# A new, finer step order in a software-pipelined graph network kernel, and another PSUM bank for the product with V

## What is computed

```
h = relu(layernorm(x));  x = x + L0(h)   # 8 Euler steps of a diffusion, folded into a polynomial
h = relu(layernorm(x));  x = x + L1(h)   # graph attention (gat): softmax over masked, leaky s1 + s2, times W h
h = relu(layernorm(x));  x = x + L2(h)   # attention over 256 edges (edge), 4 heads, gather and scatter by node
h = relu(layernorm(x));  x = x + L3(h)   # Laplacian propagation and norm (cheb), masked softmax attention
                                         # with 4 heads of 32 (att), norm, gelu FFN, norm (ffn)
```

## Time and profile before

| | |
|---|---|
| median of 3 runs | 1535.29 us (1531.87 to 1538.79) |
| profiled execution | 1538.55 us, its span 1536.8 us |
| granted TensorE clock, mean | 0.92 |
| busy: PE / DVE / ACT / POOL | 81% / 54% / 50% / 31% |
| layers part of the span | from about 454 us on |

### The profile page before, as it was taken

The page is one execution under the profiler, slowest core; times in us unless marked ns, Lnnn a source line. Parts: engine busy times, 40 slices in busy tenths (PEclk is TensorE's granted clock), DMA queues, the critical chain, the costliest instruction groups (busy, mean ns, idle before and its releaser), DMA issues. The chain is left out here.

```text
span 1536.8 us, 24908 instructions
## 1 busy us (share of the span) xinstructions
PE 1245.7 (81%) x7613; PEld 953.8 (62%) x7613; DVE 834.5 (54%) x2837; ACT 772.1 (50%) x1612; POOL 471.6 (31%) x578
## 2 busy tenths in 40 slices
PE   5899999999964576887887988888878878878754
PEld 3578788888953454665665665666656656655432
DVE  6632131322323456677668677677676676755431
ACT  4124233331102226667667667667676676665651
POOL 5012030113402223325245244244343352442222
PEclk8899999999985788999999999999999999999976
DMA  5010111101010012322312412413313224124210
GB/s 101 14 42 8 43 34 35 49 15 48 1 35 7 14 43 54 90 57 66 99 46 63 109 35 74 105 30 84 75 47 96 55 61 103 43 64 101 67 52 12
DMA packets 123742, 83.62 MB, mean 54 GB/s; under 512 B 13216, under 2 KB 106784, under 8 KB 123680
## 3 DMA queue, kind: packets, MB, share of 16 engines
q1 hardware_dynamic: 123680, 82.82, 21.1%
HBM read 28.25 MB, written 20.97 MB: 32 GB/s over the span
## 5 line engine op out<-in xcount | busy, mean ns | idle before, releaser
L1320 ACT ACTIVATE att_Es<-att_Ts,att_small 128x512 f32<-128x512 f32 x256 | 184.0, 719 | 139.3 <-DVE att_small L1501 130.5
L1501 DVE CUSTOM_DVE_ANT_0 att_Ts<-bank,mask_att 128x512 f32<-128x512 f32 x256 | 174.3, 686 | 132.2 <-PE bank L1568 131.0
L1704 PE MATMUL bank<-ident,att_Es 128*128 128x128 f32 x1024 | 168.5, 290 | 81.7 <-ACT att_PTs L1328 69.6
L1704 PEld LDWEIGHTS bank<-ident,att_Es 128*128 128x128 f32 x1024 | 122.2, 147 | 148.0 <-ACT att_Es L1320 91.3
L1328 ACT COPY att_PTs<-bank 128x512 f32<-128x512 f32 x256 | 145.7, 569 | 18.3 <-PE bank L1704 18.1
L1568 PE MATMUL bank<-K_parts,Q_parts 128*128 128x512 f32 x256 | 133.9, 533 | 3.6 <-DVE att_small L1501 3.6
L289 POOL TENSOR_SCALAR l_rs<-l_mv 128x4 f32<-128x4 f32 x16 | 6.9, 432 | 248.4 <-DVE l_mv L469 248.3
L844 PE MATMUL bank<-G,x0T 128*128 128x128 f32 x384 | 75.9, 280 | 1.2 <-DVE U2T L478 1.0
L483 DVE TENSOR_TENSOR P_row<-bank,l_bias 128x512 f32<-128x512 f32 x32 | 22.1, 691 | 99.2 <-PE bank L854 77.7
L844 PE MATMUL bank<-G,U2T 128*128 128x128 f32 x384 | 75.0, 277 | 0.0
L844 PE MATMUL bank<-G,U1T 128*128 128x128 f32 x384 | 75.0, 277 | 0.0
(11 more groups left out here) (307 smaller groups left out, 3236.0 us busy)
## 6 DMA issues: line engine op xcount, KB each, us to landing
Q_parts<-q_hi SPq DMA_DIRECT2D x128, 64.0 KB, 2.0
Q_parts<-q_lo SPq DMA_DIRECT2D x128, 64.0 KB, 2.0
K_parts<-k_hi SPq DMA_DIRECT2D x128, 64.0 KB, 2.0
K_parts<-k_lo SPq DMA_DIRECT2D x128, 64.0 KB, 2.0
l_x<-in_x SPq DMA_DIRECT2D x16, 256.0 KB, 3.0
P2T<-in_x SPq DMA_DIRECT2D x16, 256.0 KB, 4.2
x_after_l<-P2T SPq DMA_DIRECT2D x16, 256.0 KB, 2.3
gat_xin<-x_after_l SPq DMA_DIRECT2D x16, 256.0 KB, 3.2
```

What stands on the lines that cost most here:

```text
L1320: nc.scalar.activation(att_E[:, j % RING_E, :], att_T[:, j % RING_T, :], ACT.Exp, scale=-1.0, bias=att_small[:, 0, j:j + 1], accum_out=att ...
L1501: nc.vector.tensor_tensor_reduce(att_T[:, j % RING_T, :], [c0, c1][j % 2][:], k.mask_att[:, j % NT, :], -QK_SCALE, HUGE, ALU.add, ALU.min, ...
L1704: mm = nc.tensor.transpose(c2[:, cols(s)], att_E[:, i % RING_E, cols(s)], k.ident[:])
```

## The change

Only `build_layers` is touched. The steps are cut finer: a step that ran several instructions in a row becomes several steps (for example `gat_max` becomes `gat_max0` to `gat_max3`, `edge_max` four steps of one head, `ln_stats` is split into statistics and aggregation, an affine step into its two instructions, and the att steps into att_score, att_turn, att_mask, att_exp and att_copy). A step can carry a `+` in an order: it then works on the batch of one pass earlier, that is, its lag is one more. Splitting brings some waits of its own (`freed`) in front of steps that another step used to stand between. The product with V goes into b0 instead of c2, and the wait of the first transpose for `att_oT` is gone. The cut of the diff:

```diff
 ORDER = {
     "PE": """
-        att16 att0 att1 att17 att18 att2 ffn_wo att3 cheb_prop att4 gat_turn cheb_g gat_wh att5 gat_s2 ffn_turn
-        att6 ffn_up att7 ffn_down att8 gat_eturn0 edge_gather att9 cheb_x1turn gat_eturn2 cheb_q edge_x att10
-        cheb_k edge_lb att11 gat_pv edge_lcol att12 edge_den att13 edge_scatter att14 edge_out att15 cheb_v
+        att_score0 att_score1 att_turn15+ att_rows+ att_pv0+ att_pv1+ att_score2 att_turn0 ffn_wo att_score3
+        att_turn1 cheb_prop0 cheb_prop1 att_score4 att_turn2 gat_turn cheb_g gat_wh gat_s1 att_score5 att_turn3
+        gat_s2 ffn_turn att_score6 att_turn4 ffn_up0 ffn_up1 att_score7 att_turn5 ffn_down0 ffn_down1 att_score8
+        att_turn6 gat_eturn0 gat_eturn1 edge_gather0 edge_gather1 att_score9 att_turn7 cheb_x1turn gat_eturn2
+        gat_eturn3 cheb_q edge_x att_score10 att_turn8 cheb_k edge_lb0 edge_lb1 att_score11 att_turn9 gat_pv0
+        gat_pv1 edge_lcol edge_v att_score12 att_turn10 edge_den att_score13 att_turn11 edge_scatter att_score14
+        att_turn12 edge_out att_score15 att_turn13 cheb_v att_turn14
     "DVE": """
-        cheb_stats att16 edge_stats att0 att1 cheb_lo att_scale att2 gat_stats att3 ffn_y2 gat_apply att4
-        n2_apply cheb_y att5 gat_s1_out att6 gat_scores att7 n1_apply gat_max att8 ffn_y3 cheb_x1 att9 cheb_qlow
-        att10 edge_z cheb_klow edge_max att11 n3_apply edge_le att12 edge_u att13 att14 ffn_final att15 edge_x3
-        gat_x2
+        cheb_stats cheb_aggr gat_x2a+ att_mask0 gat_x2b+ edge_stats att_mask1 edge_aggr cheb_lo att_mask2
+        att_scale gat_stats ffn_y2 gat_aggr att_mask3 n2_stats n2_aggr gat_apply att_mask4 n2_apply cheb_y
+        n1_stats n1_aggr att_mask5 gat_s1_out gat_scores0 att_mask6 gat_scores1 gat_scores2 gat_scores3 gat_row1
+        n1_apply gat_row2 gat_row3 att_mask7 gat_max0 gat_max1 ffn_y3 gat_max2 att_mask8 gat_max3 n3_stats
+        cheb_x1 att_mask9 cheb_qlow edge_z att_mask10 edge_max0 edge_max1 att_mask11 edge_max2 cheb_klow n3_aggr
+        gat_rinv edge_max3 edge_le att_mask12 edge_rden edge_attn edge_u att_mask13 n3_apply att_mask14
+        att_mask15 edge_x3 att_rv ffn_final
     "ACT": """
-        att16 att17 att18 cheb_apply cheb_hi att0 att1 att2 edge_apply att3 cheb_xpT gat_hT att4 edge_hi
-        gat_wh_out att5 ffn_x2T att6 ffn_gelu att7 gat_exp att8 gat_eT0 edge_hg cheb_x1T att9 cheb_qsplit
-        edge_xz gat_eT2 cheb_ksplit att10 att11 edge_exp att12 att13 edge_yT att14 att15 cheb_vout
+        cheb_apply cheb_hi att_spread+ att_exp0 att_exp1 att_exp2 att_copy0 edge_apply att_exp3 att_copy1
+        cheb_xpT edge_hi gat_hT att_exp4 att_copy2 gat_wh_out att_exp5 att_copy3 ffn_x2T att_exp6 att_copy4
+        ffn_gelu0 ffn_gelu1 att_exp7 att_copy5 gat_exp0 gat_exp1 gat_exp2 att_exp8 att_copy6 gat_exp3 gat_eT0
+        gat_eT1 edge_hg cheb_x1T att_exp9 att_copy7 cheb_qsplit edge_xz gat_eT2 gat_eT3 att_exp10 cheb_ksplit
+        att_copy8 att_exp11 att_copy9 edge_exp att_exp12 att_copy10 att_exp13 att_copy11 edge_yT att_exp14
+        att_copy12 att_exp15 att_copy13 cheb_vout att_copy14 att_copy15
     "POOL": """
-        cheb_rstd edge_rstd ffn_res gat_rstd n2_rstd n2_affine n1_rstd ffn_b2 edge_lo gat_low n1_affine n3_rstd
-        n3_affine
+        cheb_rstd edge_rstd ffn_res gat_rstd n2_rstd n2_g n2_b n1_rstd edge_lo ffn_b2 gat_low0 gat_low1 gat_low2
+        gat_low3 n1_g n1_b n3_rstd n3_g n3_b
     "SP": """
-        load_x load_ffn cheb_res load_v stack0 stack2 stack1 stack3 store_out store_v edge_store
+        load_x load_ffn stack1+ stack3+ store_v+ load_v cheb_res edge_store+ stack0 stack2 store_out
...
+            lags = {step: LAG[STAGE_OF[step.rstrip("+")]] + step.count("+") for step in order}
...
         def ln_stats(dve, tag, n, src):
+            freed(dve, tag + "_aggr", n, NT)
...
+        def ln_aggr(dve, tag, n, last_reader):
+            freed(dve, *last_reader)
...
             def att_scale(n):
-                nc.vector.tensor_tensor(oT[:], c2[:], row_scale[:], ALU.mult).then_inc(sem("att_oT"), 1)
+                nc.vector.tensor_tensor(oT[:], b0[:], row_scale[:], ALU.mult).then_inc(sem("att_oT"), 1)
...
-                    if i == 0:
-                        freed(pe, "att_oT", n)
...
+            def att_pv(n, half):
+                if half == 0:
+                    need(pe, sem("edge_done"), min(n + 3, B) if isinstance(n, int) else n + 3)
...
-                            mm = nc.tensor.matmul(c2[r, :], vD[:, s, r], att_PT[:, h, s, :], start=(s == 0),
+                        mm = nc.tensor.matmul(b0[r, :], vD[:, s, r], att_PT[:, h, s, :], start=(s == 0),
```

More of the change, by code:

```diff
@@ L988 @@
     "gat": """
-        load_x gat_rstd gat_stats gat_hT gat_turn gat_apply gat_wh gat_wh_out gat_s2 gat_s1_out gat_scores
-        gat_low gat_exp gat_max gat_eT0 gat_eturn0 gat_eturn2 gat_eT2 gat_pv gat_x2
+        gat_turn gat_wh gat_s1 gat_s2 gat_eturn0 gat_eturn1 gat_eturn2 gat_eturn3 gat_pv0 gat_pv1 gat_stats
+        gat_aggr gat_apply gat_s1_out gat_scores0 gat_scores1 gat_scores2 gat_scores3 gat_row1 gat_row2 gat_row3
+        gat_max0 gat_max1 gat_max2 gat_max3 gat_rinv gat_x2a gat_x2b gat_hT gat_wh_out gat_exp0 gat_exp1
@@ L996 @@
+        edge_x3 edge_apply edge_hi edge_hg edge_xz edge_exp edge_yT edge_rstd edge_lo edge_store
     """.split(),
     "cheb": """
-        cheb_rstd cheb_stats cheb_apply cheb_hi cheb_lo cheb_xpT cheb_res cheb_prop cheb_g stack0 cheb_y
-        stack2 stack1 n1_rstd stack3 n1_apply n1_affine cheb_x1 cheb_x1turn cheb_x1T cheb_q cheb_qsplit
-        cheb_qlow cheb_ksplit cheb_klow cheb_k cheb_vout cheb_v store_v
+        cheb_prop0 cheb_prop1 cheb_g cheb_x1turn cheb_q cheb_k cheb_v cheb_stats cheb_aggr cheb_lo cheb_y
@@ L1003 @@
+    """.split(),
     "ffn": """
-        load_ffn att_scale ffn_res ffn_wo n2_rstd ffn_y2 n2_apply n2_affine ffn_turn ffn_x2T ffn_b2
-        ffn_gelu ffn_up n3_rstd ffn_y3 ffn_down n3_apply store_out n3_affine ffn_final
-    """.split() + [f"att{j}" for j in range(TILES, TILES + 3)],
+        ffn_wo ffn_turn ffn_up0 ffn_up1 ffn_down0 ffn_down1 att_scale ffn_y2 n2_stats n2_aggr n2_apply ffn_y3
+        n3_stats n3_aggr n3_apply ffn_final ffn_x2T ffn_gelu0 ffn_gelu1 ffn_res n2_rstd n2_g n2_b ffn_b2 n3_rstd
+        n3_g n3_b load_ffn store_out
@@ L1656, in edge_out, with cheb_prop @@
                 by_nodes(b1, YT, W["WoutT"][:]).then_inc(sem("edge_outed"), 1)
-            def cheb_prop(n):
-                ready(pe, "cheb_hlo", n)
-                freed(pe, "v_out", n)
-                for s in range(NT):
+            def cheb_prop(n, half):
+                if half == 0:
+                    ready(pe, "cheb_hlo", n)
+                    freed(pe, "v_out", n)
+                for s in (2 * half, 2 * half + 1):
                     for i, (left, right) in enumerate([(h_hi, k.lap_hi), (h_hi, k.lap_lo), (h_lo, k.lap_hi)]):
```

406 lines of the change are left out of this document (227 added, 179 removed).

## The result

The changed kernel takes 1450.67 us (median of 4 runs, 1449.96 to 1454.56), the kernel before 1537.04 beside it. The ratio is 0.9439, with a 95% interval of 0.9395 to 0.9484. The span shrinks by 88.1 us, from 1536.8 to 1448.7. It is outside the narrower band of the forecast (1463 to 1490), which had a chance of 0.5; the case that came is that rival, which had 0.17.

What follows compares the result with a forecast made beforehand. No engine is full: a pass is a chain crossing engines, TensorE nearest to full. 4.3 + 0.4 = 4.7 per pass over twelve passes, 56.4, plus 5 gives 61.4, forecast 1474 us, range 1446 to 1512.

Steps and rivals of the forecast that it cites:

- narrower band of the forecast: Whole kernel: the forecast case, 1463 to 1490 us, with a chance of 0.5.
- that rival: TensorE's clock stays up and slack in VectorE's block is used: 5.8 to 6.3 per pass, 1455 us; chance 0.17.
- Shape of the kernel: TensorE's order stays the same, so every gain or loss comes from when other engines release it.
- SyncE, 1.15: load_x goes out 2.3 us earlier, so TensorE's 1.18 wait ahead of gat_turn goes: 1.15, bounds 0 and 1.18.
- stack1, 0: SyncE's later stack1 copies still land 0.8 us ahead of score4's need: 0, or 0.7 of wait at worst.
- slower rival: stack1 lands late for score4: 1543 us with 1.2 per issue, 1607 with 1.86; chance 0.06.
- Bank b0, 0: turn0 no longer waits for att_scale but needs the later exp0: value 0, bounds -0.3 (a loss) and +0.65.
- VectorE's block, 3.15 of the 4.3: ffn_y3, n1_apply and gat_scores0 move earlier on VectorE; edge_gather starts 4.3 us earlier, SyncE's 1.15 included.
- The wait moves: Rival: VectorE waits at ffn_y3, or stack1 and gat_max1 are late; half of 4.3 lost, 1506 us; chance 0.2.
- Clock, 0.4: TensorE's clock dip at edge_gather partly goes: a quarter of 1.5 us per pass, 0.4; bounds 0 and 1.5.
- Filling and draining, 5: Filling and draining passes have parts of the gain: 5 us in all, bounds 0 and 12.
- the clock rival: TensorE's clock stays up through the gather and VectorE's slack is used: 1455 us; chance 0.17.

Runs made afterwards that it cites:

- x1: The changed kernel's finer steps only, with all orders and bank c2 as in the kernel before; 1540.66 us beside 1540.23, ratio 1.0001.
- x2: x1 with SyncE's new order only (stack1, stack3, store_v and edge_store behind the next pass's loads); 1523.81 us, ratio 0.9894.
- x9: x1 with both SyncE's new order and ffn_y3 and n1_apply early on VectorE; 1483.41 us, ratio 0.9634.
- x12: x9 with exp8 and copy6 ahead of gat_exp3 on ScalarE and mask8 ahead of gat_max3 on VectorE; 1467.57 us, ratio 0.9545.
- x4: The changed kernel with the product with V back in bank c2 and turn0's wait for att_oT; 1452.71 us, ratio 0.9459.
- x5: The changed kernel with SyncE's old order, stores and second half of the stack copies ahead of the next pass's loads; 1553.01 us, ratio 1.0111.
- x10: The changed kernel with score8 ahead of ffn_down0, att_spread ahead of cheb_apply, copy0 ahead of exp2, att_scale ahead of mask2; 1445.2 us, ratio 0.9381.
- x3: x1 with two VectorE moves: ffn_y3 between gat_max1 and gat_max2, n1_apply ahead of gat_row2; 1507.27 us, ratio 0.9799.
- x7: The changed kernel with n1_apply behind att_mask7, where the kernel before had it; 1465.54 us, ratio 0.9532.
- x8: The kernel before with three extra matmuls per pass, results unused, filling TensorE's idle time; 1527.55 us, ratio 0.9922.
- x6: The changed kernel with ffn_y3 behind gat_max3 on VectorE instead of between gat_max1 and gat_max2; 1470.37 us, ratio 0.9558.

## Why the prediction was right, and what was mis-sized

The kernels form a chain, each with one thing more, in us per pass: 60.03 with the finer steps alone (x1); 59.01 with SyncE's order (x2); 56.03 with ffn_y3 and n1_apply early (x9); 54.85 with exp8 and mask8 ahead (x12); 53.63 with all orders (x4); 53.41 with the bank (after). By the forecast's steps:

- *Shape of the kernel.* TensorE's order is unchanged, so gains could only come from when the others release it. Right: x1 alone moves nothing.
- *SyncE, 1.15.* load_x 2.3 earlier against the pass: measured 2.27. gat_turn's wait is gone, C is 1.32 shorter. Taken alone it is 1.0 (x2, 1.4 by the medians). But what it is worth depends on the rest: without it the new orders lose 7.3 (x5). The forecast never saw the ring of load, q_lo and 32 copies; it saw only the 1.18 that the ring left over in the old pass.
- *stack1, 0.* Right. The last copy went out at 963.16, 2.7 ahead of score4, and one wait of 0.4 in eleven passes is all that was lost. x10 shows how near it was: there score4 waits for it, 0.3 in the pass shown. The slower rival (1543) did not come. Its sum stretches eight issues where seven lie ahead of the last copy; with seven, 1.2 per issue gives 1005.2, just no loss.
- *Bank b0, 0.* Right: 0.2 per pass, within the bounds. turn0 waits 0.52 for exp0, and ffn_wo 0.37 for att_scale, where I had 0.1.
- *VectorE's block, 3.15 of the 4.3.* 3.67 measured in E, and x3 has it by the two moves alone. n1_apply at 1.11 was forecast at 1.08. gat_max0 and gat_max1 take 0.69 each, with 0.25 and 0.51 of waits for gat_low, 2.14 together, where I took 2.3; gat_max1 ends 13.5 behind score4 (979.38) where I had 14.1, and the gather starts 15.55 behind score4 where I had 16.2. The bound that I took, gat_eturn1, was not the last: TensorE does both gat_eturn without a wait, right behind turn6, which waits 0.40 for ScalarE's copy. The Trainium skill (SBUF — State Buffer, "SBUF: two separate sides") has whichever of VectorE and GpSimd starts first keep the shared port for its whole instruction; I used that against the change, with gat_max1 at 1.75. The trace agrees that one of the two pays. For gat_max3 it also agrees in who: it starts 0.08 behind n1_g (981.03), takes 1.75, and nothing on TensorE waits for it there. For gat_max0 and gat_max1 it differs, as far as GpSimd's spans can be read that closely: the second and third gat_low start at 977.43 and 978.64, 0.05 ahead of them, and yet gat_low is the one that takes longer, 1092 ns on average instead of the 692 of x7.
- *The wait moves.* With only the obvious moves it comes in part: x3 loses 1.5 of 3.7 at turn7, and x9 keeps 4.0 per pass against x1, where this rival had 2.2. That even this part did not come is due to exp8 and copy6 ahead of gat_exp3 (x12, 1.18 per pass), which I had only named as a thing to watch for. It is a part of the change that had no term in the sum.
- *Clock, 0.4.* This is the step that failed most in size. I took a quarter of 1.5, because ffn_down's wait of 1.4 stays. It does stay, and the clock stays up all the same. x8 prices it at 1.56 in F and 1.0 per pass in all, x9 at 1.3 for each pass with a dip; in the changed kernel F falls by 0.92, after the new wait of 0.70 for cheb_x1. The Trainium skill ("TensorE: Matmul & The Clock Gate", Part 1) has the half rate as the state that idleness brings back and activity releases, which was the side that came: the trace agrees, with 1.00 over all ten passes.
- *Filling and draining, 5.* Filling gives nothing, draining 13 behind the fifteenth gather; 12.5 together, just above the bound of 12. What shortens the draining passes, and why filling has nothing of the earlier loads, was not tried.

So the sum was 4.7 x 12 + 5 = 61.4, measured 6.3 x 12 + 12.5 = 88.1. The missing 27 are 19 in the passes and 7.5 in draining. The 1.5 per pass are 0.52 for the clock (0.92 in F against 0.4), 0.52 for VectorE's block, 0.17 for SyncE, 0.24 in G, which had no term, and 0.09 in A, B and D together. In B 0.40 is gained, in A 0.33 lost; what in the orders makes these two was not tried, nor which steps make the 1.22 between x12 and x4. The time is 5 us above the lower end of the range. It is inside because the range was drawn to take in the clock rival, not because the sum was near.

## What to carry to other kernels

Look for rings that cross the loop's edge: an engine that issues all its DMAs in a row between two events of the pass sets a floor together with the work between its first load and its first copy, and whoever shortens the rest of the pass meets it; a reordering that looked worth 1 us alone held up 7 here. When a step is moved ahead of another, check the engine that consumes both: here ScalarE's order had to follow VectorE's, or 1.5 of 3.7 us came back as a wait. Price the clock on its own with filler work ahead of the idle stretch before taking a fraction of it.

## What the runs showed of the hardware

- The length of the last idle stretch of TensorE alone does not tell whether the clock falls. 2.03 us ahead of the gather before brought 1.2 GHz (660 ns per matmul), with waits of 0.45 and 1.01 shortly ahead of it; 1.88 at the same place in x6, without those two, did not (415 ns). turn7's 1.90 brought it down in x3 (a mean of 0.97 over 742 to 1276), and in x9 in every second of eight passes with the same waits (0.99). What decides between the passes of x9 is not shown.
- Who pays when VectorE and GpSimd both work from SBUF depends on what meets. gat_low beside gat_max: gat_low 1092 ns on average, gat_max mostly 690. gat_low beside n1_apply: gat_low 692, n1_apply 663 instead of 342. Whether n1_apply stands ahead of the two small row steps or behind them decides between the two.
